# Layer norms and router statistics of a four-layer transformer kernel: from whole-tensor passes to one statistics and one scaling instruction per 128-row tile

## The chip, the cores and the metric

The kernel runs on one core of a Trainium2 chip. The metric is the device time of one execution in microseconds, and a kernel's time is the median of several executions. TensorE (PE) multiplies matrices, VectorE (DVE), ScalarE (ACT) and GpSimd (POOL) work on tiles of 128 partitions, and SyncE (SP) issues the transfers between memory and the on-chip buffer.

## The reference

Input x is 8 x 256 rows of 128 float32 numbers, with a context of the same shape. Four layers follow each other; each adds a gated attention over the context and a gated feed-forward part, both of a layer norm of x:

```python
def _layernorm(x, axis=-1, eps=1e-05):
    m = jnp.mean(x, axis=axis, keepdims=True)
    v = jnp.var(x, axis=axis, keepdims=True)
    return (x - m) / jnp.sqrt(v + eps)
...
    x = x + jnp.tanh(g_xattn[0]) * _L0_xattn_ref(_layernorm(x, axis=-1), ctx_1024, ctx_1024)
...
    x = x + jnp.tanh(g_ffn[3]) * _L3_ffn_ref(_layernorm(x, axis=-1), L3_ffn_r1_w, L3_ffn_r1_b, L3_ffn_r2_w, L3_ffn_w_up, L3_ffn_w_down, L3_ffn_a_up, L3_ffn_a_down)
```

Layer 0's feed-forward part is a chain of six attention nodes with a layer norm of its own (eps 1e-6) at its end. Layer 1's attention norms its input once more. The feed-forward parts of layers 1 and 2 are quantised. Layer 3's is a mixture of 32 experts, whose router sees each row beside six statistics of it:

```python
    def _stats(x):
        mean = x.mean(-1, keepdims=True)
        std = jnp.std(x, axis=-1, keepdims=True, ddof=1)
        mn = x.min(-1, keepdims=True)
        mx = x.max(-1, keepdims=True)
        l2 = jnp.linalg.norm(x, axis=-1, keepdims=True)
        sp = (jnp.abs(x) < 1e-06).astype(x.dtype).mean(-1, keepdims=True)
        return jnp.concatenate([mean, std, mn, mx, l2, sp], -1)
```

## The kernel before

x stays in the buffer for the whole run as X, 128 partitions x 16 tiles x 128 columns (NT = 16, D = 128), one row of x per partition and tile. Each part of a layer is a stage, written once for each engine as a function (l0f_dve, l1x_dve, ffn_dve, x_dve, moe_dve and their counterparts). Stages are separated by barriers that all five engines reach. Inside a stage the order of the work is written by hand, and engines wait on semaphores. On VectorE, link() adds to a semaphore when an instruction ends and waits for it before the next starts; an instruction without link() is followed by the next one with no wait.

A stage begins with its loads, issued by SyncE right after the barrier, and with the norm of X into Qf on VectorE. Meanwhile GpSimd and ScalarE fill blank rows of the query and key buffers (L342 and L347) once all loads have landed. TensorE then transposes Qf and goes on with the stage.

The norm is ln_dve, called nine times: at the start and the end of layer 0's node chain, twice in layer 1's attention, once in each of the two quantised feed-forward parts, in layer 2's and layer 3's attention, and in the router's stage. It makes five passes over 2048 numbers a partition (L311, L313, L314, L315, L317), and calls rstd_dve (L287 to L296), which asks ScalarE for a square root (L301) and improves its inverse by one Newton step. The norm of layer 0's attention is made from another layout by other code and doesn't call ln_dve. The router's stage then computes the mean, the deviation and the 2-norm of every row of Qf with six more passes (L1923 to L1930), asks ScalarE for the roots, and goes on with the minimum (L1932), the maximum (L1933) and the count of small values.

Of the kernel before, what the change touches and what calls it, by code (L numbers as in the profile page):

```python
# [18 lines left out]
P = 128  # L19
B, S, D = 8, 256, 128  # L20
NT = B * S // P
# [119 lines left out]
def flamingo(nc, T, out):  # L141
    with ExitStack() as ctx:
        def sb(name, shape, dt=F32, scope=ctx):
            return scope.enter_context(nc.sbuf_tensor(name, shape, dt))
# [35 lines left out]
        rest = sb("rest", [P, 2 * S])  # L180
        st1 = sb("st1", [P, 256])
# [121 lines left out]
        def bc(ap, shape):  # L303
            return ap.to_broadcast(shape)

        def ln_dve(v, src, dst, tmp, eps):

            d = v.eng
            sh = [P, NT, D]
            m = st1[:, 0:NT]  # L310
            v.link(d.tensor_reduce(m, src, AX, ALU.add))  # L311
            v.link(d.tensor_scalar(m, m, -1.0 / D, None, ALU.mult))
            v.link(d.tensor_tensor(dst, src, bc(m.unsqueeze(2), sh), ALU.add))  # L313
            v.link(d.tensor_tensor(tmp, dst, dst, ALU.mult))  # L314
            v.link(d.tensor_reduce(m, tmp, AX, ALU.add))  # L315
            rstd_dve(v, m, NT, eps, 1.0 / D)
            v.link(d.tensor_tensor(dst, dst, bc(st3[:, 0:NT].unsqueeze(2), sh), ALU.mult))  # L317

# [660 lines left out]
        def l0f_dve(v):  # L982
            d = v.eng
            ln_dve(v, X[:], Qf[:], O[:], 1e-5)
# [11 lines left out]
            ln_dve(v, Qf[:], Qf[:], O[:], 1e-6)  # L996
# [231 lines left out]
        def l1x_dve(v):  # L1228
            d = v.eng
            ln_dve(v, X[:], Qf[:], O[:], 1e-5)  # L1230
            ln_dve(v, Qf[:], Qf[:], O[:], 1e-5)
# [137 lines left out]
        def ffn_dve(v, Q):  # L1369
# [4 lines left out]
            ln_dve(v, X[:], Qf[:], O[:], 1e-5)  # L1374
# [252 lines left out]
        def x_dve(v, k):  # L1627
            d = v.eng
            L = attentions[k]
            ln_dve(v, X[:], Qf[:], O[:], 1e-5)  # L1630
# [285 lines left out]
        def moe_dve(v):  # L1916
            d = v.eng
            ln_dve(v, X[:], Qf[:], O[:], 1e-5)
            sh = [P, NT, D]
            mean, dev = st[:, :, 0:1], col[:, 2, :]  # L1920

            v.link(d.memset(st[:], 1.0))
            v.link(d.tensor_reduce(st[:, :, 0], Qf[:], AX, ALU.add))  # L1923
            v.link(d.tensor_scalar(st[:, :, 0], st[:, :, 0], 1.0 / D, None, ALU.mult))
            v.link(d.tensor_tensor(O[:], Qf[:], bc(mean, sh), ALU.subtract))
            v.link(d.tensor_tensor(O[:], O[:], O[:], ALU.mult))
            v.link(d.tensor_reduce(col[:, 2], O[:], AX, ALU.add))
            v.link(d.tensor_scalar(col[:, 2], col[:, 2], 1.0 / (D - 1), None, ALU.mult))
            v.link(d.tensor_tensor(O[:], Qf[:], Qf[:], ALU.mult))
# [280 lines left out]
```

## Time and profile before

| | us |
|---|---|
| median of 3 runs | 1986.42 (1985.71 to 1988.87) |
| the profiled execution | 1996.73 |
| its span | 1994.8 |
| TensorE busy | 1377.0 |
| VectorE busy | 1362.2 |
| ScalarE busy | 752.7 |
| GpSimd busy | 410.0 |

The span goes from the first to the last instruction of the profiled execution, whose own time includes what lies around it. Busy times add up what an engine works anywhere in the span; they don't say which engine the others wait for in a given stage.

### The profile page before, as it was taken

To read this page: it belongs to the slowest core of one execution; us is meant where nothing else is said; L and a number is where in the kernel's file an instruction comes from. 1 tells how busy PE (TensorE), PEld (TensorE's weight loads), DVE (VectorE), ACT (ScalarE), POOL (GpSimd) and SP (SyncE) were. 2 spreads that over 40 slices of the span, in tenths; PEclk is the share of its full clock that TensorE was granted. 3 is DMA by queue.
4 is the path that set the end of the run, shared out by engine and by line. 5 is a ranking of instruction groups with operands and counts; after the bars stand their busy time and mean duration, and the time that the engine had idled before them with its cause. 6 is when DMAs were issued, how large, how long until landed. Compare 5 with 4: busy or idle time off the path is not lost. (4 is left out here: it accounts for less than half of the span.)

```text
span 1994.8 us, 32063 instructions
## 1 busy us (share of the span) xinstructions
PE 1377.0 (69%) x12362; PEld 955.8 (48%) x12362; DVE 1362.2 (68%) x2054; ACT 752.7 (38%) x1092; POOL 410.0 (21%) x588
## 2 busy tenths in 40 slices
PE   0798189999999933888888834299514887120997
PEld 0565156666666621555665522166404454110897
DVE  5564457777777766676777778476587675869565
ACT  1255147667777731333333312145321365100110
POOL 6243232222222100222222200434102100000221
PEclk9898589999999975899999965589757799555899
DMA  2242322222232201000000000222001320110342
GB/s 69 49 68 35 92 81 88 83 89 89 85 91 85 89 24 41 1 1 1 1 1 1 1 11 0 48 60 53 12 0 32 65 50 19 61 21 0 93 146 86
DMA packets 115183, 95.88 MB, mean 48 GB/s; under 512 B 44180, under 2 KB 98516, under 8 KB 114132
## 3 DMA queue, kind: packets, MB, share of 16 engines
q1 hardware_dynamic: 114020, 92.63, 17.5%
q8 instruction: 96, 1.57, 0.3%
q0 software_dynamic: 1024, 1.32, 0.3%
q14 instruction: 43, 0.35, 0.1%
HBM read 33.23 MB, written 3.15 MB: 18 GB/s over the span
## 5 line engine op out<-in xcount | busy, mean ns | idle before, releaser
L586 ACT ACTIVATE Pt<-bank 128x1024 f32<-128x1024 f32 (+1 forms) x384 | 366.1, 953 | 181.0 <-PE bank L530 179.3
L642 DVE TENSOR_REDUCE l0f_Mf<-bank 128x4 f32<-128x1024 f32 x192 | 234.5, 1222 | 108.1 <-PE bank L509 108.0
L550 PE MATMUL bank<-Pt,V 128*32 128x256 f32 (+1 forms) x3072 | 199.0, 378 | 10.1 <-POOL Pt L391 8.9
L1102 POOL TENSOR_TENSOR Psum<-Pt 128x512 f32<-128x512 f32 x64 | 81.1, 1267 | 321.7 <-ACT Pt L1221 321.7
L550 PEld LDWEIGHTS bank<-Pt,V 128*32 128x32 f32 x3072 | 82.2, 112 | 82.8 <-issue 29.4
L832 PE MATMUL bank<-ident,Qf 128*128 128x128 f32 x64 | 14.1, 414 | 154.4 <-SPq L242 91.5
L391 POOL TENSOR_SCALAR_AFFINE_SELECT Pt<-Pt 128x512 f32<-128x512 f32 x128 | 81.5, 637 | 181.0 <-ACT Pt L586 181.0
L1269 DVE RECIPROCAL st<-bank 128x256 f32<-128x256 f32 x64 | 111.9, 1749 | 6.9 <-PE bank L1182 6.8
L1244 DVE TENSOR_TENSOR qk_lo<-bank,qk_hi 128x512 fp32r<-128x512 f32 x64 | 44.1, 689 | 103.2 <-ACT qk_hi L1213 103.2
L530 PE MATMUL bank<-l0f_QK 64*128 64x256 f32 x768 | 97.6, 333 | 19.8 <-DMA l0f_QK<-l0f_NMrow 19.2
L407 POOL CAST parts<-nodes 128x256 fp32r<-128x256 f32 x96 | 38.0, 396 | 305.1 <-PE bank L481 305.1
L642 DVE TENSOR_REDUCE l2x_Mf<-bank 128x4 f32<-128x1024 f32 x64 | 76.8, 1220 | 32.7 <-PE bank L509 32.7
L1764 POOL DMA_INDIRECT xg<-s_rows,sloti x32 | 29.3, 916 | 330.1 <-PEq L242 237.9
L1221 ACT ACTIVATE Pt<-bank 128x1024 f32<-128x1024 f32 x64 | 65.5, 1024 | 77.7 <-PE bank L1165 77.7
L530 PEld LDWEIGHTS bank<-l0f_QK 64*128 64x128 f32 x768 | 57.9, 187 | 73.2 <-ACT Pt L586 34.0
L832 PEld LDWEIGHTS bank<-ident,Qf 128*128 128x128 f32 x64 | 12.9, 224 | 155.3 <-SPq L242 92.2
L1177 PE MATMUL bank<-Pt,V 128*64 128x256 f32 x512 | 70.3, 395 | 19.6 <-DVE AnT L1271 19.6
L509 PE MATMUL bank<-l0f_QK 63*128 63x256 f32 x768 | 78.6, 283 | 5.8 <-DVE l0f_Mf L642 5.8
L1213 ACT CAST qk_hi<-bank 128x512 fp32r<-128x512 f32 x64 | 37.5, 586 | 115.0 <-PE bank L1121 115.0
L1248 DVE TENSOR_REDUCE Mx<-bank 128x4 f32<-128x1024 f32 x64 | 77.8, 1216 | 1.0 <-PE bank L1140 1.0
L590 ACT COPY OT<-bank 128x512 f32<-128x512 f32 x96 | 56.2, 586 | 54.6 <-PE bank L550 54.6
L559 PE MATMUL bank<-ident,OT 128*128 128x128 f32 x384 | 63.3, 289 | 13.0 <-ACT OT L590 5.5
(363 smaller groups left out, 3383.7 us busy)
## 6 DMA issues: line engine op xcount, KB each, us to landing
l0f_QK<-l0f_Z SPq DMA_DIRECT2D x288, 128.0 KB, 2.4
l2x_QK<-l2x_Z SPq DMA_DIRECT2D x96, 128.0 KB
Wup<-in_L_upT SPq DMA_DIRECT2D x16, 512.0 KB, 3.5
l0x_QK<-l0x_Z SPq DMA_DIRECT2D x48, 128.0 KB
Wdn<-in_L_downT SPq DMA_DIRECT2D x16, 256.0 KB, 3.6
Aup<-in_L_aupT SPq DMA_DIRECT2D x16, 128.0 KB, 3.5
l0f_QK<-l0f_NMrow SPq DMA_DIRECT2D x96, 4.0 KB
WeT<-in_L_WeT SPq DMA_DIRECT2D x1, 1280.0 KB
```

Of the source, the lines that this page charges most:

```text
L391: e.affine_select(diagonal, diagonal, [[0, 2], [0, 2], [1, P]], ALU.is_ge, 0.0, base=0, channel_multiplier=-1).then_inc(L.kept, 1)
L509: last = pe.matmul(bank[L.first(j) + x][:, t * S:t * S + w], L.QK[rs, u % L.ring, j, 0, t * P:(t + 1) * P], L.QK[rs, u % L.ring, j, 1, 0:w ...
L530: last = pe.matmul(bank[2 + x][:, t * S:t * S + S - q0], L.QK[rs, u % L.ring, j, 1, t * P:(t + 1) * P], L.QK[rs, u % L.ring, j, 0, q0:S], ...
L550: last = pe.matmul(bank[4][32 * x:32 * x + 32, o + q0:o + S], Va[:, 2 * n + k, 4 * j + x, :], Pp[:, (f + x // 2) % 4, x % 2, k * S:k * S + ...
L559: last = pe.transpose(b[:, (2 * t + k) * P:(2 * t + k + 1) * P], OT[:, k, t * P:(t + 1) * P], ident[:, :])
L586: act.activation(Pp[:, g % 4, :, 0:w], banks[:, 2:4, 0:w], ACT.Exp, scale=L.scale).then_inc(exp_done, 1)
L642: d.tensor_reduce(m, A.rearrange("p h (t k) -> p h t k", t=2), AX, ALU.max).then_inc(max_done, 1)
L1102: e.tensor_tensor(Psum[:, q % 2], Pp[:, q % 4, :, 0:S], Pp[:, q % 4, :, S:2 * S], ALU.add).then_inc(key_sum, 1)
L1177: pe.matmul(y[64 * x:64 * x + 64, 0:S], Vr[:, u % 8, k, 2 * j + x, :], Pp[:, g % 4, x, k * S:(k + 1) * S], start=(k == 0), stop=(k == 1), ...
L1221: act.activation(Pp[:, g % 4], banks[:, 2:4, :], ACT.Exp, scale=float(DH1) ** -0.5).then_inc(l1_exp, 1)
L1248: d.tensor_reduce(m[:, :, 2 * j:2 * j + 2].rearrange("p t h -> p h t"), banks[:, 0:2, :].rearrange("p h (t k) -> p h t k", t=2), AX, ALU.m ...
L1269: d.reciprocal(st1[:], y[:, S:2 * S]).then_inc(pair_done, 1)
```

## The change

A norm now begins with `moments`: one BN_STATS instruction for each of the 16 tiles, which writes six numbers a row (for the even and for the odd columns apart: a count, their mean, and their sum of squared deviations), and five small instructions that combine them to twice the mean and the variance. After rstd_dve, which is the same, one tensor_scalar a tile subtracts the mean and multiplies by the inverse root; both operands are read from a column of numbers, one for each partition. The 16 instructions of either kind have no wait between them. The norm no longer uses the scratch tensor O. The router's mean, deviation and 2-norm come from the same `moments` and five small instructions.

```diff
+        bn = sb("bn", [P, NT, 6])
...
-        def ln_dve(v, src, dst, tmp, eps):
+        def moments(v, src):
...
             d = v.eng
-            sh = [P, NT, D]
-            m = st1[:, 0:NT]
-            v.link(d.tensor_reduce(m, src, AX, ALU.add))
-            v.link(d.tensor_scalar(m, m, -1.0 / D, None, ALU.mult))
-            v.link(d.tensor_tensor(dst, src, bc(m.unsqueeze(2), sh), ALU.add))
-            v.link(d.tensor_tensor(tmp, dst, dst, ALU.mult))
-            v.link(d.tensor_reduce(m, tmp, AX, ALU.add))
-            rstd_dve(v, m, NT, eps, 1.0 / D)
-            v.link(d.tensor_tensor(dst, dst, bc(st3[:, 0:NT].unsqueeze(2), sh), ALU.mult))
...
+            for t in range(NT):
+                last = d.bn_stats(bn[:, t, :], src[:, t, :])
+            v.link(last)
+            m, dif, var = st1[:, 0:NT], st1[:, NT:2 * NT], st1[:, 2 * NT:3 * NT]
+            d.tensor_tensor(m, bn[:, :, 1], bn[:, :, 4], ALU.add)
+            d.tensor_tensor(dif, bn[:, :, 1], bn[:, :, 4], ALU.subtract)
+            v.link(d.tensor_tensor(var, bn[:, :, 2], bn[:, :, 5], ALU.add))
+            v.link(d.scalar_tensor_tensor(out=dif, in0=dif, scalar=0.25, in1=dif, op0=ALU.mult, op1=ALU.mult))
+            v.link(d.scalar_tensor_tensor(out=var, in0=var, scalar=1.0 / D, in1=dif, op0=ALU.mult, op1=ALU.add))
+            return m, var
+
+        def ln_dve(v, src, dst, eps):
+
+            d = v.eng
+            m, var = moments(v, src)
+            d.tensor_scalar(m, m, 0.5, None, ALU.mult)
+            rstd_dve(v, var, NT, eps, 1.0)
+            for t in range(NT):
+                last = d.tensor_scalar(dst[:, t, :], src[:, t, :], m[:, t:t + 1], st3[:, t:t + 1], ALU.subtract,
+                                       ALU.mult)
+            v.link(last)
...
         def moe_dve(v):
             d = v.eng
-            ln_dve(v, X[:], Qf[:], O[:], 1e-5)
-            sh = [P, NT, D]
-            mean, dev = st[:, :, 0:1], col[:, 2, :]
-
+            ln_dve(v, X, Qf, 1e-5)
             v.link(d.memset(st[:], 1.0))
-            v.link(d.tensor_reduce(st[:, :, 0], Qf[:], AX, ALU.add))
-            v.link(d.tensor_scalar(st[:, :, 0], st[:, :, 0], 1.0 / D, None, ALU.mult))
-            v.link(d.tensor_tensor(O[:], Qf[:], bc(mean, sh), ALU.subtract))
-            v.link(d.tensor_tensor(O[:], O[:], O[:], ALU.mult))
-            v.link(d.tensor_reduce(col[:, 2], O[:], AX, ALU.add))
-            v.link(d.tensor_scalar(col[:, 2], col[:, 2], 1.0 / (D - 1), None, ALU.mult))
-            v.link(d.tensor_tensor(O[:], Qf[:], Qf[:], ALU.mult))
-            v.link(d.tensor_reduce(col[:, 3], O[:], AX, ALU.add))
+            m, var = moments(v, Qf)
+            v.link(d.tensor_scalar(st[:, :, 0], m, 0.5, None, ALU.mult))
+            v.link(d.tensor_scalar(col[:, 2], var, float(D) / (D - 1), None, ALU.mult))
+            v.link(d.tensor_tensor(col[:, 3], st[:, :, 0], st[:, :, 0], ALU.mult))
+            v.link(d.tensor_tensor(col[:, 3], col[:, 3], var, ALU.add))
+            v.link(d.tensor_scalar(col[:, 3], col[:, 3], float(D), None, ALU.mult))
             d.drain().then_inc(ln_ask, 1)
```

On VectorE, the norm at the start of layer 1's feed-forward part stands in a row before as follows (st is any of the small buffers st1 to st3, Qf the normed rows, O the scratch tensor):

```order
L311 TENSOR_REDUCE st<-X 128x16
L312 TENSOR_SCALAR st<-st 128x16
L313 TENSOR_TENSOR Qf<-X,st 128x2048
L314 TENSOR_TENSOR O<-Qf 128x2048
L315 TENSOR_REDUCE st<-O 128x16
L287 TENSOR_SCALAR st<-st 128x16
L288 COPY st<-st 128x16
L292 RECIPROCAL st<-st 128x16
L293 TENSOR_TENSOR st<-st 128x16
L294 TENSOR_TENSOR st<-st 128x16
L295 TENSOR_SCALAR st<-st 128x16
L296 TENSOR_TENSOR st<-st 128x16
```

It ends with one more pass, L317. In the changed kernel the same place reads, on the same engine (line numbers of the changed kernel; bn holds the six numbers a row and tile):

```order
L311 BN_STATS bn<-X 128x6 x16
L314 TENSOR_TENSOR st<-bn 128x16
L315 TENSOR_TENSOR st<-bn 128x16
L316 TENSOR_TENSOR st<-bn 128x16
L317 SCALAR_TENSOR_TENSOR st<-st 128x16
L318 SCALAR_TENSOR_TENSOR st<-st 128x16
L325 TENSOR_SCALAR st<-st 128x16
L288 TENSOR_SCALAR st<-st 128x16
L289 COPY st<-st 128x16
L293 RECIPROCAL st<-st 128x16
```

Four passes of 2048 and one small instruction became 16 statistics and six small ones ahead of the root; behind it, the pass L317 became 16 instructions L328. Next, VectorE in the router's stage before, from the setting of the statistics' buffer on (col holds columns of per-row numbers):

```order
L1922 MEMSET st 128x128
L1923 TENSOR_REDUCE st<-Qf 128x16
L1924 TENSOR_SCALAR st<-st 128x16
L1925 TENSOR_TENSOR O<-Qf,st 128x2048
L1926 TENSOR_TENSOR O<-O 128x2048
L1927 TENSOR_REDUCE col<-O 128x16
L1928 TENSOR_SCALAR col<-col 128x16
L1929 TENSOR_TENSOR O<-Qf 128x2048
L1930 TENSOR_REDUCE col<-O 128x16
L1932 TENSOR_REDUCE st<-Qf 128x16
```

And there in the changed kernel, with the norm's last instructions ahead:

```order
L328 TENSOR_SCALAR Qf<-X,st 128x128 x16
L1928 MEMSET st 128x128
L311 BN_STATS bn<-Qf 128x6 x16
L314 TENSOR_TENSOR st<-bn 128x16
L315 TENSOR_TENSOR st<-bn 128x16
L316 TENSOR_TENSOR st<-bn 128x16
L317 SCALAR_TENSOR_TENSOR st<-st 128x16
L318 SCALAR_TENSOR_TENSOR st<-st 128x16
L1930 TENSOR_SCALAR st<-st 128x16
L1931 TENSOR_SCALAR col<-st 128x16
L1932 TENSOR_TENSOR col<-st 128x16
L1933 TENSOR_TENSOR col<-col,st 128x16
```

Six passes of 2048 and two small instructions ahead of the minimum became 16 statistics and ten small ones; the minimum and all that follows stay. No other engine's instructions change.

## Rows read from the trace of the kernel before

**Rows 1.** The page, busy time, share of the span and instructions of each engine.

```profile
PE 1377.0 (69%) x12362; PEld 955.8 (48%) x12362; DVE 1362.2 (68%) x2054; ACT 752.7 (38%) x1092; POOL 410.0 (21%) x588
```

**Rows 2.** Windows: length, busy us of PE, PEld, DVE, ACT, POOL, clock, DMA share, GB/s.

```profile
210.00:242.00 32.00, 0.00 (x0) 0.00 (x0) 18.20 (x20) 5.38 (x6) 10.07 (x18) 0.50 0.50 140
...
743.00:774.00 31.00, 0.00 (x0) 0.00 (x0) 29.35 (x27) 1.92 (x4) 8.13 (x4) 0.50 0.31 104
...
1694.00:1736.00 42.00, 0.00 (x0) 0.00 (x0) 38.95 (x35) 1.73 (x3) 0.00 (x0) 0.52 0.19 73
```

**Rows 3.** Timeline, layer 1's feed-forward: start us, duration us, instruction.

```profile
1165.65 2.29 DVE L311 TENSOR_REDUCE st<-X 128x16 f32<-128x2048 f32 x1
...
1167.97 0.17 DVE L312 TENSOR_SCALAR st<-st 128x16 f32<-128x16 f32 x1
...
1175.15 0.17 DVE L287 TENSOR_SCALAR st<-st 128x16 f32<-128x16 f32 x1
...
1175.66 1.28 ACT L301 ACT_TABLE_LOAD   x1 [11.17 <-DVEq L289]
...
1178.33 2.29 DVE L317 TENSOR_TENSOR Qf<-Qf,st 128x2048 f32<-128x2048 f32 x1
...
1180.76 2.29 DVE L1377 TENSOR_REDUCE top<-Qf 128x1 f32<-128x2048 f32 x1
```

**Rows 4.** Timeline of VectorE, router's stage.

```profile
1709.62 2.29 DVE L1923 TENSOR_REDUCE st<-Qf 128x16 f32<-128x2048 f32 x1
...
1724.09 2.29 DVE L1932 TENSOR_REDUCE st<-Qf 128x16 f32<-128x2048 f32 x1
1726.29 2.28 DVE L1933 TENSOR_REDUCE st<-Qf 128x16 f32<-128x2048 f32 x1
...
1760.02 1.59 DVE L1972 MAX8 t<-pr 128x8 f32<-128x32 f32 x16
```

**Rows 5.** Groups of instructions of VectorE: busy us, mean ns of one, idle before.

```profile
L1932 DVE TENSOR_REDUCE st<-Qf 128x16 f32<-128x2048 f32 x1 | 2.3, 2287 | 0.1
...
L1972 DVE MAX8 t<-pr 128x8 f32<-128x32 f32 x16 | 1.6, 177 | 0.0
...
L1967 DVE TENSOR_REDUCE col<-pr 128x16 f32<-128x512 f32 x1 | 0.7, 685 | 0.8 <-ACT pr L1886 0.8
...
L1439 DVE TENSOR_SCALAR diag<-ident,sw,gates 128x128 f32<-128x128 f32 x2 | 0.7, 345 | 0.1
```

**Rows 6.** Timeline, start of layer 3's attention.

```profile
1506.48 2.29 DVE L311 TENSOR_REDUCE st<-X 128x16 f32<-128x2048 f32 x1
...
1514.62 5.57 POOL L342 CAST l2x_QK<-l2x_rowk 128x2048 fp32r<-128x2048 f32 x3 [6.96 <-DMA l2x_rowk<-in_c_rows]
...
1516.57 1.80 DVE L288 COPY st<-st 128x16 f32<-128x16 f32 x1
...
1520.87 2.29 DVE L317 TENSOR_TENSOR Qf<-Qf,st 128x2048 f32<-128x2048 f32 x1
```

**Rows 7.** Timeline, start of layer 0's node chain.

```profile
231.23 2.29 DVE L317 TENSOR_TENSOR Qf<-Qf,st 128x2048 f32<-128x2048 f32 x1
...
232.46 4.92 POOL L342 CAST l0f_QK<-l0f_rowk 128x1024 fp32r<-128x1024 f32 x4 [12.96 <-DMA V<-in_L_ffn_We]
...
233.55 2.92 DVE L988 TENSOR_TENSOR ewbe<-ew,beT 128x1 f32<-128x1 f32 x6
```

**Rows 8.** Timeline, start of layer 2's attention.

```profile
1269.69 2.29 DVE L1654 TENSOR_TENSOR X<-X,bx 128x2048 f32<-128x2048 f32 x1
...
1273.91 7.13 POOL L1589 TENSOR_SCALAR padr<-padi 16x2048 fp32r<-16x2048 int32 x1 [7.55 <-issue]
```

**Rows 9.** Timeline, start of layer 1's attention.

```profile
745.86 1.89 POOL L1091 TENSOR_TENSOR Esel<-Esel,ident 128x1024 bf16<-128x1024 bf16 x1
746.22 1.56 DVE L312 TENSOR_SCALAR st<-st 128x16 f32<-128x16 f32 x1
...
750.14 3.87 DVE L314 TENSOR_TENSOR O<-Qf 128x2048 f32<-128x2048 f32 x1
```

More of the change, by code:

```diff
@@ L995, in l0f_dve @@
             v.barrier()
-            ln_dve(v, Qf[:], Qf[:], O[:], 1e-6)
+            ln_dve(v, Qf, Qf, 1e-6)
             sh_ = [P, NT, D]
@@ L1229, in l1x_dve @@
             d = v.eng
-            ln_dve(v, X[:], Qf[:], O[:], 1e-5)
-            ln_dve(v, Qf[:], Qf[:], O[:], 1e-5)
+            ln_dve(v, X, Qf, 1e-5)
+            ln_dve(v, Qf, Qf, 1e-5)
             loaded(v, 8)
@@ L1373, in ffn_dve @@
             top = {"apply_absolute_value": Q.gated}
-            ln_dve(v, X[:], Qf[:], O[:], 1e-5)
+            ln_dve(v, X, Qf, 1e-5)
             loaded(v, len(ffn_loads(Q)))
@@ L1629, in x_dve @@
             L = attentions[k]
-            ln_dve(v, X[:], Qf[:], O[:], 1e-5)
+            ln_dve(v, X, Qf, 1e-5)
             loaded(v, len(x_loads(k)))
@@ L1917, in moe_dve @@
             d = v.eng
-            ln_dve(v, X[:], Qf[:], O[:], 1e-5)
-            sh = [P, NT, D]
-            mean, dev = st[:, :, 0:1], col[:, 2, :]
+            ln_dve(v, X, Qf, 1e-5)
             v.link(d.memset(st[:], 1.0))
-            v.link(d.tensor_reduce(st[:, :, 0], Qf[:], AX, ALU.add))
-            v.link(d.tensor_scalar(st[:, :, 0], st[:, :, 0], 1.0 / D, None, ALU.mult))
-            v.link(d.tensor_tensor(O[:], Qf[:], bc(mean, sh), ALU.subtract))
-            v.link(d.tensor_tensor(O[:], O[:], O[:], ALU.mult))
-            v.link(d.tensor_reduce(col[:, 2], O[:], AX, ALU.add))
-            v.link(d.tensor_scalar(col[:, 2], col[:, 2], 1.0 / (D - 1), None, ALU.mult))
-            v.link(d.tensor_tensor(O[:], Qf[:], Qf[:], ALU.mult))
-            v.link(d.tensor_reduce(col[:, 3], O[:], AX, ALU.add))
+            m, var = moments(v, Qf)
[4 more added lines that the diff above has]
+            v.link(d.tensor_scalar(col[:, 3], col[:, 3], float(D), None, ALU.mult))
             d.drain().then_inc(ln_ask, 1)
```

## The prediction

> **What bounds the kernel now.** The page comes first [rows 1]: TensorE is busy 69% of the span and VectorE 68%, and neither share says what a layer norm is worth. So I cut the span at the stage borders and read it by windows [rows 2]. In the stretches where the norms stand TensorE is idle: 0.00 us of work between 743 and 774 us and between 210 and 242 us, 0.00 between 1694 and 1736 us. In two of the three VectorE is busy nearly throughout (29.35 of 31 us, 38.95 of 42 us). There VectorE alone sets the end: every microsecond taken off it is a microsecond of the kernel. In 210 to 242 it works 18.20 of 32 us, so something else ends that stretch. I then went through the timeline of all nine calls of ln_dve and asked of each which engine arrives last at the barrier that follows.
>
> Six calls end a stretch alone: the one after the node flow (722 us), both of the first cross stage (744 and 761 us), both feed-forward ones (1166 and 1434 us) and the router's (1694 us). [rows 3] is one of them: each instruction starts 0.03 to 0.04 us after the end of the one before, nothing is hidden under it, and the maximum of L1377 follows at once. The eighth (1506 us) ends its part too, but shares it with GpSimd. Two don't count: the call at 218 us ends at 233.5, while GpSimd's casts, which had to wait for the weights, begin only at 232.46 [rows 7]; and the one at 1251 us is over long before GpSimd's L1589, which starts at 1273.91 and takes 7.13 us while VectorE's last work ends at 1271.98 [rows 8].
>
> **The change part by part.** *Removed from a norm.* From the first instruction to L287 it is 1175.15 - 1165.65 = 9.50 us [rows 3], for two sums, a subtraction and a product over 2048 elements, and a small one. L317 is 2.29 + 0.03 = 2.32 us. Together 11.82 us. What lies between, rstd_dve, stays: 1178.33 - 1175.15 = 3.18 us with ScalarE's table load.
>
> *Sixteen statistics instructions.* The trace has none, so I bound them. They have no semaphore between them, and what such a chain costs is its start-to-start distance, not the duration. Two unlinked sums show it: L1932 starts at 1724.09 and L1933 at 1726.29, 2.20 us apart, though each lasts 2.29 [rows 4]. The slope is 1.04 ns an element (2.287 us for 2048 less 0.685 for 512, over 1536 [rows 5]), so 0.067 of the 2.20 us is fixed. The 16 maxima of 32 elements take 1.59 us, 177 ns each but (1.59 - 0.18)/15 = 94 ns apart, which is 33 + 61 [rows 4, 5]. So 128 elements at one a cycle give 0.133 + 0.067 = 0.20 us, and 16 of them 3.20 + 0.09 of tail + 0.03 = 3.32 us. Lower bound: 0.19 with the maxima's 61 ns. Upper bound: two cycles an element, as if one pass took the mean and one the variance, 0.333 us each. I take the low end: the nearest rows, a sum and an 8-fold maximum over one input, both run at one element a cycle.
>
> *The small ones.* Two unlinked on 16 values at 0.067 + 0.017 = 0.08, three linked at 0.21 (0.17 of L312 [rows 3] and 0.04 to the next), one unlinked 0.08: 0.87 us. First instruction to L287: 4.19 us instead of 9.50, a gain of 5.31.
>
> *Sixteen tensor_scalar with two pointer operands.* One of this very shape and operands stands in the trace: L1439, 345 ns with a wait on either side [rows 5]. In a chain I take off the 2.29 - 2.20 = 0.09 of overlap: 0.26 us, times 16, + 0.12 = 4.28 us. It replaces 2.32. This half of the change loses 1.96 us a norm: the 16 fixed parts and 32 pointer loads cost more than the saved pass of 2048. Bounds: 0.26 and, with no overlap, 0.345.
>
> Net per exposed norm: 5.31 - 1.96 = 3.35 us; six of them 20.1.
>
> *Router's statistics.* L1923 starts at 1709.62 and L1932 at 1724.09 [rows 4]: 14.47 us for six passes and two small ones. New: 3.32 for the statistics, 0.79 for two unlinked and three linked small ones, five linked small ones at 0.21, 0.1 of drain: 5.26. Gain 9.2 us, all on the path (ScalarE's root is asked for earlier, and VectorE still has its minima, maxima and counts to do behind it).
>
> *Contention with GpSimd.* Sums run undisturbed beside GpSimd's work, while VectorE's two-input, copy and tensor_scalar instructions take turns with it: at 746 us L312 lasts 1.56 instead of 0.17 us and L314 3.87 instead of 2.29 [rows 9], 2.97 us together. The new statistics have one input and should go through, until (746.22 - 2.32) + 3.32 = 747.2; then the small ones wait for L1091 until 747.75 and for one more turn of 1.89: 2.4 us. Gain 0.5 more.
>
> At 1506 us the turns cost more. The load-bound casts L342 start at 1514.62 and last 5.57 us [rows 6]; L288 waits 1.80 there. New: the moments end at 1506.48 + 4.19 = 1510.67, the root without table load (3.18 - 1.28) leads to 1512.57, and (1514.62 - 1512.57)/0.26 = 8 of the 16 products are done when the casts begin. The six small ones of L988 in 2.92 us beside three casts show that two unlinked instructions pass per cast [rows 7], so some 4 are left at 1520.6 and the norm ends near 1521.8 instead of 1523.2: gain 1.4. Bounds: 0, and 1523.2 - (1512.57 + 4.28) = 6.3 if these products don't take turns at all.
>
> *The two covered calls.* At 218 us GpSimd's first cast waits for L317 until 233.52, 1.06 us [rows 7]; the norm is now over by 231, gain 1.0. Were that cover gone, this norm would be worth 3.35. At 1251 us the products now fall on GpSimd's casts instead of into the gap between them and L1589; each turn delays GpSimd by some 0.2 us, and GpSimd ends that stretch: loss 0.6, between 0 and 2.3 (if L1654, 2.29 us, gets in ahead of GpSimd's copy) [rows 8].
>
> What is late next in the first cross stage are the loads. The DMA engines are busy 0.31 of the 31 us there [rows 2], 9.6 us, so they are through long before the new barrier at about 767.
>
> **Sum.** 20.1 + 9.2 + 0.5 + 1.4 + 1.0 - 0.6 = 31.6 us. The profiled execution took 1996.73 us, 10.3 above the median of the three runs, with the same stretches; nothing in the sum depends on TensorE. Profile: 1965.1. Median: 1986.4 - 31.6 = **1954.8 us**.
>
> **A rule that speaks against it.** The Trainium skill, page "VectorE: DVE Perf Modes", section "The DRAIN you can't avoid", says that the next instruction starts only when the pipe has emptied, semaphore or not, and that the number of instructions is what to minimise; its section on the trn2 errata adds that many small tiles pay the fixed cost each. This trace disagrees for unlinked instructions, 94 ns apart at 177 ns each. The page "Vector Engine (DVE) Microarchitecture Reference", section 5.2, gives about 75 ns an instruction after overlap; an estimate from it would be 0.133 + 0.075 = 0.208 us for one statistics instruction, 1 us more over the kernel.
>
> **Rivals.** (a) *The chain doesn't overlap.* Statistics 0.286 us each (the sum's 2.286 less 1920 x 1.042 ns), products 0.345. A norm: 16 x 0.286 + 0.03 + 0.87 + 16 x 0.345 + 0.03 = 11.04 against 11.82, gain 0.8; router 7.8; the casts at 1514 then catch nearly all products, gain 0 there. 4.7 + 7.8 + 0.5 + 1.0 - 0.6 = 13.4: 1973.0 us. The maxima [rows 4, 5] speak against it; that a pointer load may end the overlap speaks for its half. By the Trainium skill's drain rule above, this is what would come. Chance 0.10.
> (b) *Two cycles an element.* 16 x 0.133 = 2.13 us more in seven exposed places, and the 1.4 at 1506 us goes: 31.6 - 16.3 = 15.3, 1971.1 us. No row excludes it. Chance 0.11.
> (c) *More than forecast.* The products pass GpSimd freely, 6.3 instead of 1.4 us at 1506, and nothing is lost at 1251: 1986.4 - 31.6 - 4.9 - 0.6 = 1949.3 us. The waits of L288 speak against. Chance 0.10.
> (d) *Slower.* The statistics instruction has a long fixed part of its own. It decides at 31.6/(7 x 16) = 0.28 us more each, from 0.48 us a piece; at 0.6 us it is 112 x 0.40 = 45 us, 2000 us. Nothing in the trace is near that (the short instructions stand at 0.15 to 0.35 us isolated), but the instruction is unseen. Chance 0.04.
>
> My case: 0.65, own range 1948 to 1962. Under 0.2%, 4 us, a measurement of this kernel can't tell a difference; a statistics instruction of 0.44 to 0.52 us, between (b) and (d), would land there, 0.03 out of these two. The range takes in (a), (b) and (c): 1947 to 1974. Faster 0.94, same 0.03, slower 0.03.
>
> **What would show it.** In the profile after: BN_STATS mean under 0.3 us, 16 of them in 3.3 us; L328 mean about 0.345, 16 in 4.3; first statistics to L288 4.2 us; TensorE's first transpose of the gated feed-forward 3.4 us earlier after its stage's start; the router's stretch from the norm's end to the minima 5.3 us; the start-up to 242 us only 1 us shorter. Wrong it would be above all if 16 statistics take 5 us or more.

## The result, and the profile after

The changed kernel takes 1957.13 us (median of 4 executions, 1952.78 to 1959.63) against 1987.53 of before in the same rounds: a ratio of 0.9838, 95% interval 0.9818 to 0.9858, or 28 to 36 us less. A second series on another occasion gave 1958.34 us and 0.9848 (0.9812 to 0.9885). The prediction was 1954.8. Of all executions reported here one, of the kernel that takes the statistics twice, stood at a granted clock of 0.62 and took 2287.92 us; it is left out of that kernel's median and ratio.

The page's busy line of the kernel after, beside [rows 1]:

```profile
PE 1365.0 (70%) x12362; PEld 947.0 (49%) x12362; DVE 1325.6 (68%) x2360; ACT 753.7 (39%) x1092; POOL 413.4 (21%) x588
```

VectorE has 306 instructions more and 36.6 us of work less. Its share of the span is 68% as before, since the span has shrunk with it.

The timeline of VectorE in the kernel after, layer 1's feed-forward, the counterpart of [rows 3]:

```profile
1149.06 3.19 DVE L311 BATCH_NORM_STATS2 bn<-X 128x6 f32<-128x128 f32 x16
1152.29 0.18 DVE L314 TENSOR_TENSOR st<-bn 128x16 f32<-128x16 f32 x1
...
1153.20 0.17 DVE L288 TENSOR_SCALAR st<-st 128x16 f32<-128x16 f32 x1
...
1156.38 4.19 DVE L328 TENSOR_SCALAR Qf<-X,st 128x128 f32<-128x128 f32 x16
1160.72 2.29 DVE L1386 TENSOR_REDUCE top<-Qf 128x1 f32<-128x2048 f32 x1
```

From the first statistics to L288 it is 1153.20 - 1149.06 = 4.14 us; the same piece was 9.50 us. The 16 instructions L328, called the products from here on, take 4.19 us in a row.

The groups of VectorE in the kernel after, each form apart: busy us, mean ns of one, idle before.

```profile
L328 DVE TENSOR_SCALAR Qf<-X,st 128x128 f32<-128x128 f32 x112 | 40.9, 442 | 0.3
...
L311 DVE BATCH_NORM_STATS2 bn<-X 128x6 f32<-128x128 f32 x112 | 22.3, 278 | 1.0
...
L328 DVE TENSOR_SCALAR Qf<-Qf,st 128x128 f32<-128x128 f32 x32 | 8.4, 338 | 0.1
```

A statistics instruction lasts 278 ns, yet 16 of them end after 3.19 us: they start (3.19 - 0.28)/15 = 0.194 us apart. The product lasts 338 ns where nothing disturbs it, and starts (4.19 - 0.34)/15 = 0.257 us apart. The 442 ns of the group on X come from the two attention norms that meet GpSimd's casts, where the 16 products take 10.84 us (layer 2) and 9.14 us (layer 3).

The timeline of VectorE in the router's stage of the kernel after, beside [rows 4]:

```profile
1675.13 3.19 DVE L311 BATCH_NORM_STATS2 bn<-Qf 128x6 f32<-128x128 f32 x16
...
1680.04 0.17 DVE L1934 TENSOR_SCALAR col<-col 128x16 f32<-128x16 f32 x1
1680.36 2.29 DVE L1936 TENSOR_REDUCE st<-Qf 128x16 f32<-128x2048 f32 x1
```

The statistics up to the minimum take 1680.36 - 1675.13 = 5.23 us instead of 14.47.

The first rows of layer 1's attention in the kernel after, where [rows 9] showed VectorE taking turns with GpSimd:

```profile
735.45 3.19 DVE L311 BATCH_NORM_STATS2 bn<-X 128x6 f32<-128x128 f32 x16
738.68 0.68 DVE L314 TENSOR_TENSOR st<-bn 128x16 f32<-128x16 f32 x1
...
739.57 1.76 DVE L317 SCALAR_TENSOR_TENSOR st<-st 128x16 f32<-128x16 f32 x1
```

The 16 statistics pass undisturbed; two small ones wait for their turn, 0.50 + 1.59 = 2.09 us instead of 2.97.

Read stretch by stretch over the same instructions of both traces, from the first instruction of the norm to the first work of TensorE or GpSimd that waits for it (in layer 2's attention, to GpSimd's first copy ahead of TensorE; for the norm that ends the node chain, to the next stage's first load), in us:

| stretch | before | after | gain | forecast |
|---|---|---|---|---|
| start-up norm to the transposes | 23.86 | 22.84 | 1.0 | 1.0 |
| norm that ends the node chain | 22.10 | 18.62 | 3.5 | 3.35 |
| both norms of layer 1's attention | 30.42 | 22.59 | 7.8 | 7.2 |
| gated feed-forward | 29.61 | 26.15 | 3.5 | 3.35 |
| layer 2's attention | 30.50 | 30.46 | 0.0 | -0.6 |
| plain feed-forward | 28.75 | 25.28 | 3.5 | 3.35 |
| layer 3's attention | 16.94 | 15.43 | 1.5 | 1.4 |
| router's norm and statistics | 41.66 | 28.95 | 12.7 | 12.55 |
| sum | | | 33.5 | 31.6 |

The two profiled spans differ by more, 1994.8 - 1951.1 = 43.7 us. The other 10.2 lie in stretches whose code is the same: 5.9 ahead of the first norm, 4.8 and 1.2 in the flows of layers 2 and 3, 0.3 in layer 1's, less 1.9 given back in the node chain. Before's profiled execution lies 9 us above its median and after's 4 below, which is enough for that part; most likely it belongs to the two executions and not to the change.

### The profile page after: what moved, and what is told of

It reads as the page before. It is cut to its first block and busy times, and to the rows that moved or that the text cites. A ratio compares the mean times of both kernels' runs of the same rounds, so it can differ in the third digit from the quotient of the medians.

```text
span 1951.1 us, 32369 instructions
## 1 busy us (share of the span) xinstructions
PE 1365.0 (70%) x12362; PEld 947.0 (49%) x12362; DVE 1325.6 (68%) x2360; ACT 753.7 (39%) x1092; POOL 413.4 (21%) x588
## 5 line engine op out<-in xcount | busy, mean ns | idle before, releaser
L559 PE MATMUL bank<-Pt,V 128*32 128x256 f32 (+1 forms) x3072 | 194.8, 372 | 11.1 <-POOL Pt L400 10.0
L418 POOL TENSOR_TENSOR parts<-nodes,parts 128x256 fp32r<-128x256 f32 x96 | 70.2, 731 | 7.7
```

Source lines behind the costliest of these rows:

```text
L418: e.tensor_tensor(lo, node, hi.bitcast(F32), ALU.subtract).then_inc(L.parts_in, 1)
L559: last = pe.matmul(bank[4][32 * x:32 * x + 32, o + q0:o + S], Va[:, 2 * n + k, 4 * j + x, :], Pp[:, (f + x // 2) % 4, x % 2, k * S:k * S + ...
```

## The experiments

Each was timed beside the kernel before on one chip, in four series on different chips; so medians of different series are best compared by their ratios to before. Where a few microseconds decide I read TensorE's idle gap around a norm, from the end of its last work ahead of the norm to its first work behind it. Over the same code the gap mostly repeats to 0.03 us between executions (cross stage, that is the node chain's last norm and both of layer 1's attention: 42.14, 42.17, 42.15; gated feed-forward 26.98, 27.00, 27.00), with one exception of 0.4 us (42.53 in the cross stage of the kernel with the covered norms as before); in layer 2's attention, where loads end late, it moves by a microsecond. Whole executions of one kernel spread by 10 to 20 us.

**The router alone.** The edit, against the changed kernel: every call of the norm goes to the old function, the router's part stays as changed.

```diff
-            ln_dve(v, X, Qf, 1e-5)
+            ln_dve(v, X[:], Qf[:], O[:], 1e-5)
```

> The router's statistics as in the changed kernel, all layer norms as before. The prediction priced this half at 9.2 us, the changed kernel's trace gives it 14.47 - 5.23 = 9.2: about 1978 us against 1987.5. If the instructions of a chain did not overlap it would be 7.8. If the two halves of the change help each other (one shortens what the other waits for), this run and the norms' 24 us do not add up to the 30 us measured. In the trace: L323's group absent, the sixteen statistics of the router in 3.2 us, and the norms' L312 to L317 with their durations of before.

Measured: 1983.74 us, ratio 0.9965 (0.994 to 0.999), 2 to 12 us faster. The router's gap is 33.35 instead of 42.59 us, 9.24 less, to the hundredth what the changed trace gave; the cross stage's 53.79 and the feed-forward's 30.45 stay as in the kernel before (53.80, 30.45). The overlap-free 7.8 is out. From 33.35 the norm takes the router's gap to the changed kernel's 29.88, another 3.47, so the halves add up: they don't help each other.

**Whole-tensor passes.**

```diff
-            d.tensor_scalar(m, m, 0.5, None, ALU.mult)
+            v.link(d.tensor_scalar(m, m, 0.5, None, ALU.mult))
+            v.link(d.tensor_tensor(dst[:], src[:], bc(m.unsqueeze(2), sh), ALU.subtract))
             rstd_dve(v, var, NT, eps, 1.0)
-            for t in range(NT):
-                last = d.tensor_scalar(dst[:, t, :], src[:, t, :], m[:, t:t + 1], st3[:, t:t + 1], ALU.subtract,
-                                       ALU.mult)
-            v.link(last)
+            v.link(d.tensor_tensor(dst[:], dst[:], bc(st3[:, 0:NT].unsqueeze(2), sh), ALU.mult))
```

> The statistics instruction stays; subtraction and product are two passes over all 2048 elements again, one ahead of the root and one behind it. Theory of the prediction: sixteen instructions cost 4.2 us in the changed kernel's trace, two passes 2 x 2.32 = 4.65 us, of which none lies under ScalarE's root because the subtraction stands ahead of it; so this kernel is 0.4 us slower than the changed one at each of six or seven exposed norms, and about 1960 us. Rival: the sixteen fixed parts and 32 pointer loads make 'one instruction a tile' a loss (it looks like one if only the product pass of 2.32 us is compared); then this kernel is faster than the changed one, at or below 1955.

Measured: 1958.5 us, 0.9859 (0.9824 to 0.9894), not to be told from the changed kernel by its time. The first matmul behind each kernel's gated feed-forward norm, with TensorE's idle time before it in brackets; first the kernel after, then this one:

```profile
1175.39 0.82 PE L1501 MATMUL bank<-identb,xq 128*128 128x128 bf16 x6 [26.98 <-SPq L243]
```

```profile
1176.60 0.60 PE L1500 MATMUL bank<-identb,xq 128*128 128x128 bf16 x4 [27.53 <-SPq L243]
```

The whole passes cost 0.55 us more a norm (0.56 in the plain feed-forward, 1.69 over the three norms of the cross stage), of which some 0.1 is the link behind the small L325's counterpart. So the one instruction a tile is worth a little, and the statistics are worth nearly all: the 1.96 us that the prediction booked as a loss of this half is the product alone, and the subtraction's 2.32 that goes with it was booked with the moments.

**Every instruction linked to the one before.**

```diff
             for t in range(NT):
-                last = d.bn_stats(bn[:, t, :], src[:, t, :])
-            v.link(last)
+                v.link(d.bn_stats(bn[:, t, :], src[:, t, :]))
```

and the same for the products.

> Same instructions as the changed kernel, but a semaphore wait on the one before between every two statistics and every two products. Theory of overlap: the distance grows from 0.194 to 0.276 + 0.035 = 0.31 us for a statistics instruction and from 0.257 to 0.339 + 0.035 = 0.37 for a product, 15 x 0.117 + 15 x 0.117 = 3.5 us a norm, six exposed norms 21 us, the router 1.8, the norm at 1478 us about 1.5: some 24 us more than the changed kernel, 1981 us. Rival, that the next instruction starts only when the one before has left the pipe, link or no link: only the semaphore's 0.035 us is added, 30 x 0.035 = 1.05 us a norm and 0.5 in the router, some 7 us in all, 1964.

Measured: 1990.05 us, 1.001 (0.9988 to 1.0033). Its timeline of VectorE, gated feed-forward:

```profile
1158.88 5.21 DVE L311 BATCH_NORM_STATS2 bn<-X 128x6 f32<-128x128 f32 x16
...
1168.22 6.08 DVE L327 TENSOR_SCALAR Qf<-X,st 128x128 f32<-128x128 f32 x16
1174.45 2.29 DVE L1384 TENSOR_REDUCE top<-Qf 128x1 f32<-128x2048 f32 x1
```

Sixteen statistics take 5.21 instead of 3.19 us and sixteen products 6.08 instead of 4.19, which is 0.329 and 0.383 us apart instead of 0.194 and 0.257. The gaps grow by 3.92 (gated), 3.93 (plain), 5.96 (router), 10.12 (cross stage) and, from stage start, 3.3 and 0.6 to 1.2 in layers 3 and 2: 28 us, where 24 were expected. Without the overlap of unlinked instructions the whole change would be worth about 5. The rival's 7 us is out. The rule of the Trainium skill, page "VectorE: DVE Perf Modes", section "The DRAIN you can't avoid", that chaining instructions without semaphores saves nothing, does not hold here: 0.194 against 0.329 us apart. The same section says beside it that an instruction that isn't held starts earlier, and that is what the trace shows. The median lies 33 us over the changed kernel, some 5 more than the gaps say (and 9 over the 1981 expected); the last experiments are about such remainders.

**The statistics twice.**

```diff
+            for t in range(NT):
+                last = d.bn_stats(st2[:, 128 + 6 * t:134 + 6 * t], src[:, t, :])
             for t in range(NT):
                 last = d.bn_stats(bn[:, t, :], src[:, t, :])
```

> Sixteen more statistics instructions ahead of each set, into a buffer that nobody reads (extra work only). If they are on the path and 0.194 us apart, each exposed set adds 16 x 0.194 = 3.1 us: seven of them 21.7, and 1 to 1.5 us at the attention norm that meets GpSimd's casts; the start-up and the norm at 1231 us add nothing. So about 22 to 24 us over the changed kernel, 1980 us. If the real price were 0.276 us each (no overlap between independent ones), 31 us. If much less than 20 appears, the norms are less exposed than the stretches say.

Measured: 1990.79 us (median of 11), ratio 0.9998 (0.9971 to 1.0025), which by the ratio is about 1988 us, where 1980 was expected. Its timeline in the gated feed-forward (the view ends after three of the second sixteen), and its first matmul behind:

```profile
1146.25 3.19 DVE L311 BATCH_NORM_STATS2 st<-X 128x6 f32<-128x128 f32 x16
1149.35 0.66 DVE L313 BATCH_NORM_STATS2 bn<-X 128x6 f32<-128x128 f32 x3
...
1175.67 1.14 PE L1503 MATMUL bank<-identb,xq 128*128 128x128 bf16 x9 [30.08 <-SPq L243]
```

1149.35 - 1146.25 = 3.10 us for sixteen, and the gap grows by 3.10 (30.08 - 26.98): all of them are on the path. Likewise 3.10 in the plain feed-forward and 6.20 in the router. In the cross stage it is 7.21 and not 9.3, because the moments' small instructions now come after GpSimd has finished and the 2.09 us of turns vanish: 9.30 - 2.09 = 7.21. With 2.8 in layer 3's stage the stretches add 22, as expected. The time rose by about 31, so some 9 us lie elsewhere.

**The covered norms as before.**

```diff
+            if k == 2:
+                ln_old(v, X[:], Qf[:], O[:], 1e-5)
+            else:
+                ln_dve(v, X, Qf, 1e-5)
```

and the old norm, here named ln_old, at start-up too.

> The norms at the start-up and ahead of the third attention stage as before the change, all else as changed. The prediction calls both covered, the first by GpSimd's casts (worth 1.0 us), the second by GpSimd's last transposition (worth -0.6, 0.0 measured in the changed trace). So +1 us on the changed kernel, that is no difference in the median, and TensorE's gaps there 37.7 and 33.6 us long as in the kernel before. If each were exposed, +3.5 us each, +7. For the second stage: if the sixteen small products taking turns cost GpSimd time, its gap is shorter here than in the changed kernel (37.4).

Measured, with the changed kernel in the same rounds:

> The changed kernel once more, on the same chip and in the same rounds as the three that follow, because executions of one kernel lie up to 20 us apart here and go with the granted clock (0.01 of it is 14 us). Expected: 1957 again, ratio 0.984 or a little over; TensorE's idle gaps around the norms 218 us in sum, of before 251.

The changed kernel 1958.34 us, 0.9848 (0.9812 to 0.9885); with the two old norms 1961.08 us, 0.9855 (0.9819 to 0.9891): no difference beyond the measurement. The start-up's gap is 38.04 against 37.03 and 36.74, so 1.0 to 1.3 us, as the covering casts allow. Layer 2's attention takes from its first instruction to TensorE's first 31.45 us with the old norm and 32.01 and 32.61 with the new. Counted from GpSimd's first cast, which moves by up to 1.2 us with the loads, it is 22.96 against 23.38 and 23.43. But the kernel before and the one with the router alone, both with the old norm there, have 23.81 and 23.28, so a difference between the norms is not shown.

**Subtraction under ScalarE's root.** The whole passes, but with the subtraction behind the request for the root and ahead of the wait for it:

```diff
             d.drain().then_inc(ln_ask, 1)
+            if meanwhile:
+                meanwhile()
             d.wait_ge(ln_answer, v.count("ln"))
...
+            def meanwhile():
+                v.link(d.tensor_tensor(dst[:], src[:], bc(m.unsqueeze(2), sh), ALU.subtract))
```

> The statistics as changed; the subtraction is one pass of 2048 elements issued while ScalarE takes the root, and one product pass follows. VectorE waits 1.68 us for ScalarE where a table must be loaded, so 2.32 us of subtraction cost 0.64 there, and the product pass saves 4.22 - 2.32 = 1.90: 1.3 us less than the changed kernel in each of the four norms with a table load (both feed-forward, the node one's follower and the router's), about nothing in the others: -5 us, 1952. If VectorE's time is all that counts (no overlap with ScalarE), it is +0.4 a norm as with both passes behind each other.

Measured: 1963.58 us, 0.9864 (0.9818 to 0.9909). The gaps give 0.97 us a norm in both feed-forwards and the router. In the cross stage they give 0.3: 0.97 for the norm that ends the node chain, less 0.68 for the two of layer 1's attention, where ScalarE has no table to load and the root is there early. The overlap is there, 0.3 less than expected: the root's answer is taken up 0.79 us later instead of 0.64, and one more link costs 0.12. Layer 3's attention gains 3.0 us (12.46 from stage start against 15.43 and 15.45): the last pass gets in after one turn. Layer 2's loses 3.2 to 3.8. Its timeline there:

```profile
1241.98 9.45 POOL L354 CAST l2x_QK<-l2x_rowk 128x2048 fp32r<-128x2048 f32 x3 [7.39 <-DMA l2x_rowk<-in_c_rows]
1243.99 1.79 DVE L1665 TENSOR_SCALAR bx<-bx,gates 128x128 f32<-128x128 f32 x1
1245.82 3.87 DVE L1666 TENSOR_TENSOR X<-X,bx 128x2048 f32<-128x2048 f32 x1
...
1260.35 7.13 POOL L1601 TENSOR_SCALAR padr<-padi 16x2048 fp32r<-16x2048 int32 x1 [7.08 <-issue]
```

The three casts take 9.45 us and not 5.57, since whole VectorE passes of 2.29 us now fall between them, and GpSimd ends this stretch. That is more than the 2.3 us that the prediction gave as its upper bound for the changed kernel here. The median misses the expected 1952 by some 11 us; its six executions fall into 1954.2 to 1957.4 and 1969.8 to 1972.4, and the profiled one, of the upper three, has the longer last segment described below.

**The product shared with ScalarE.**

```diff
+        DVE_TILES = 10
...
+            a.eng.wait_ge(ln_ask, a.count("ln"))
+            for t in range(DVE_TILES, NT):
+                last = a.eng.activation(Qf[:, t, :], src[:, t, :], ACT.Identity, scale=st3[:, t:t + 1],
+                                        bias=st1[:, 4 * NT + t:4 * NT + t + 1])
+            last.then_inc(ln_answer, 1)
...
+            v.link(d.scalar_tensor_tensor(out=st1[:, 4 * NT:5 * NT], in0=m, scalar=-1.0, in1=st3[:, 0:NT],
+                                          op0=ALU.mult, op1=ALU.mult))
+            d.drain().then_inc(ln_ask, 1)
-            for t in range(NT):
+            for t in range(DVE_TILES):
...
+            d.wait_ge(ln_answer, v.count("ln"))
```

> The products are shared: VectorE takes ten tiles, ScalarE six (multiply and add with a column each), and VectorE waits for ScalarE at the end. VectorE saves 6 x 0.257 = 1.54 us, and one linked small instruction and the hand-over add about 0.4. So 1.1 us less an exposed norm, 8 us in all, 1949, if ScalarE's six take under 2.6 us. Rival: ScalarE needs over 0.45 us a tile with the hand-over or loads another table, and the norm is longer than before its division: a gain of nothing or a loss.

Measured: 1954.49 us, 0.9829 (0.9787 to 0.9872). Its timeline of ScalarE, gated feed-forward:

```profile
1146.29 2.42 ACT L310 ACTIVATE Qf<-X,st 128x128 f32<-128x128 f32 x6 [1.41 <-DVEq L339]
1148.72 1.28 ACT L1561 ACT_TABLE_LOAD   x1
1150.02 0.20 ACT L1561 ACTIVATE clip<-clip 128x2 f32<-128x2 f32 x1
```

Six tiles take 2.42 us, less than VectorE's ten. The gap shrinks by 1.21 in the plain feed-forward and 1.22 in the router, a little more than the 1.1 expected. In the gated one it shrinks by 0.06: the table for the clip's factors (L1561) was loaded while VectorE multiplied, and now comes behind ScalarE's share, so the barrier waits for ScalarE instead. Over the three norms of the cross stage it shrinks by 2.43, where 3.3 were expected: 1.2 for each of the first two and nothing for the third, behind which ScalarE loads a table for the gate in the same way:

```profile
753.90 1.28 ACT L1233 ACT_TABLE_LOAD   x1
755.20 0.20 ACT L1233 ACTIVATE g<-g 128x1 f32<-128x1 f32 x1
```

TensorE starts at 755.50. With 1.4 in layer 3's stage and 1.0 to 1.5 in layer 2's it is some 7.5 us in all.

**A form for each place.**

```diff
+            ln_dve(v, X, Qf, 1e-5, "wait" if Q.gated else "split")
...
+            ln_dve(v, X, Qf, 1e-5, "wait" if k == 3 else "split")
```

where wait is the subtraction under the root, split the shared product; start-up and router stay as changed.

> At each norm the form whose stretch was shortest so far: the shared product (ten tiles VectorE, six ScalarE) after the node flow, in the first cross stage, in the third attention stage and in the plain feed-forward stage; the subtraction under ScalarE's root in the gated feed-forward and the fourth attention stage; start-up and router as in the changed kernel. From TensorE's gaps of the two experiments against the changed kernel: 2.44 + 1.0 + 1.23 + 0.98 + 3.0 = 8.7 us less, gap of the router 29.9 as in the changed one and with it the clock of the stage after it as there: 1957.5 - 8.7 = 1949. Rival: the clock takes back a part in another stage, 1950 to 1960.

Measured: 1945.35 us (1942.74 to 1956.28), ratio 0.9782 (0.9757 to 0.9808), the lowest median of all: 43 us under before, where the changed kernel has 31. The gaps are 39.69 in the cross stage, 26.02, 25.17 and 29.88; layer 3's stage is 1.4 us shorter than in the changed kernel and not 3.0, layer 2's no shorter (32.14): 6.0 us by the stretches, where 8.7 were expected. In layer 3's stage the casts began 7.93 us after the stage's start, ahead of the last small instruction, which had to wait; with the same form they had begun 8.17 us after it, just behind that instruction, in the kernel with the subtraction under the root everywhere:

```profile
1482.29 7.62 POOL L378 CAST l2x_QK<-l2x_rowk 128x2048 fp32r<-128x2048 f32 x3 [6.75 <-DMA l2x_rowk<-in_c_rows]
1482.40 1.81 DVE L299 TENSOR_TENSOR st<-st 128x16 f32<-128x16 f32 x1
1484.24 3.92 DVE L344 TENSOR_TENSOR Qf<-Qf,st 128x2048 f32<-128x2048 f32 x1
```

So a quarter of a microsecond in the landing of a load decided over 1.6 us there. The median lies 12 to 13 us under the changed kernel's two (11 to 13 by the ratios), more than the stretches account for. And by the stretches this kernel saves less than the product shared everywhere (7.5); that its median is 9 us lower (the intervals of the two ratios overlap) goes with the clock behind the router, the subject of the next part.

**Where the remainders come from.** The stretches of the shared product said some 7.5 us less than the changed kernel and the median shows 4; doubled statistics said +22 and show about +31. Windows of three kernels after the router's gap: the second 10 us of the stage, 20 us around the start of the experts' matmuls, and the whole rest; columns as in [rows 2]. The kernel after (gap 29.88):

```profile
1702.28:1712.28 10.00, 9.29 (x40) 5.84 (x40) 0.00 (x0) 3.06 (x4) 0.00 (x0) 0.83 0.00 0
1802.28:1822.28 20.00, 17.34 (x82) 15.71 (x83) 7.45 (x20) 2.97 (x8) 4.51 (x5) 0.60 0.19 63
...
1692.28:1951.10 258.82, 158.33 (x978) 135.74 (x978) 173.10 (x352) 26.66 (x78) 29.40 (x32) 0.78 0.22 67
```

The shared product (gap 28.66):

```profile
1687.22:1697.22 10.00, 9.32 (x18) 2.64 (x16) 0.00 (x0) 3.05 (x4) 0.00 (x0) 0.54 0.00 0
1787.22:1807.22 20.00, 11.70 (x46) 10.32 (x47) 7.23 (x16) 2.48 (x6) 4.87 (x5) 0.50 0.06 12
...
1677.22:1949.80 272.58, 171.41 (x978) 144.50 (x978) 173.18 (x352) 26.64 (x78) 29.32 (x32) 0.73 0.21 63
```

The same 978 matmuls take 272.58 us instead of 258.82. In the kernel after, TensorE's granted clock is at 0.83 in the second ten microseconds, mostly at 2.4 GHz; with the shared product it has fallen to 0.54, nearly all of it at 1.2 GHz (this is called the early fall below), so that only 18 matmuls get done instead of 40, and the experts' work starts 5.6 us later and at the lower clock. Three runs ask whether the length of the gap decides this, or chance. The first two add passes to the router's stretch, the third shares the router's product too:

```diff
+            v.link(d.tensor_reduce(st2[:, 128:128 + NT], Qf[:], AX, ALU.add))
```

```diff
+            for n in (NT, NT, 12):
+                v.link(d.tensor_reduce(st2[:, 128:128 + n], Qf[:, 0:n], AX, ALU.add))
```

```diff
-            ln_dve(v, X, Qf, 1e-5, "plain")
+            ln_dve(v, X, Qf, 1e-5)
```

> The kernel with the shared product and one more pass of 2.3 us in the router's stretch, a sum over 2048 elements that nobody reads (extra work only). In the profiles so far TensorE's granted clock after the router's stretch takes one of two courses over the same instructions: where the gap was 29.9, 30.4, 33.4 or 42.6 us the expert stage is 12 to 14 us shorter than where it was 28.7, 28.9, 35.8 or 36.1. Theory: this goes with the length of the gap, by kernel and not by chance. Then here, with a gap of 28.7 + 2.3 = 31.0, the extra work makes the kernel faster: +2.3 - 13, from 1954.5 to about 1944, the last segment (from the router's norm on) 285 instead of 296 us. Rival, that the course is drawn anew in each execution: +2.3, 1957.

Measured: 1953.89 us, 0.9809 (0.9789 to 0.9828), where 1944 was expected; gap 30.98; 261.5 us from the first matmul to the end.

> The changed kernel with three more passes in the router's stretch, sums over 2048, 2048 and 1536 elements that nobody reads (extra work only), 2.3 + 2.3 + 1.7 = 6.3 us, which puts the gap at 29.9 + 6.2 = 36.1 us, among those with the longer expert stage. Theory, that the course of the clock goes with the gap's length: +6.2 + 12 = 18 us on the changed kernel, about 1976, the last segment 302 us instead of 283.6. Rival, that it is drawn by chance: +6.2, 1964, segment 290.

Measured: 1973.54 us, 0.9915 (0.9898 to 0.9933), 15.8 over the mean of the changed kernel's two medians, or 13 to 15 by the ratios; gap 36.31, 268.5 us to the end.

> The kernel with a form by place, its router norm too with the product shared between VectorE and ScalarE. By the stretches alone this is 1.2 us faster (router's gap 28.7 instead of 29.9), 1944. Theory that the clock's course after the router goes with the gap's length: at 28.7 us the clock falls some 10 us into the stage and comes back 20 us later, as in the profiles with 28.7, 28.9 and 36 us, +13.5, so 1945.4 - 1.2 + 13.5 = 1958. Rival, the course is drawn by chance in each execution: 1944.

Measured: 1952.42 us, 0.9806 (0.9782 to 0.9829), between the theory's 1958 and the rival's 1944. It is 7 us slower than the same kernel with the plain router norm (the intervals of the two ratios overlap), although its stretches are 1.2 us shorter; gap 28.66, 264.1 us to the end. Windows of these three after the router's gap, the same stretches. The one more pass:

```profile
1702.18:1712.18 10.00, 9.32 (x30) 4.99 (x30) 0.00 (x0) 3.05 (x4) 0.00 (x0) 0.79 0.00 0
...
1692.18:1953.70 261.52, 161.07 (x978) 137.96 (x978) 173.06 (x352) 26.64 (x78) 29.32 (x32) 0.77 0.21 66
```

The three more passes on the changed kernel:

```profile
1715.77:1725.77 10.00, 9.32 (x17) 2.66 (x16) 0.00 (x0) 3.06 (x4) 0.00 (x0) 0.51 0.00 0
...
1705.77:1974.30 268.53, 168.09 (x978) 141.53 (x978) 173.15 (x352) 26.66 (x78) 29.41 (x32) 0.74 0.21 64
```

The form by place with the router's product shared too:

```profile
1697.73:1707.73 10.00, 9.32 (x18) 2.64 (x16) 0.00 (x0) 3.06 (x4) 0.00 (x0) 0.55 0.00 0
...
1687.73:1951.80 264.07, 163.19 (x978) 137.40 (x978) 173.07 (x352) 26.66 (x78) 29.41 (x32) 0.75 0.21 65
```

Over all fourteen profiles the fall follows the gap without exception:

| router's gap, us | clock in the second 10 us | first matmul to end, us |
|---|---|---|
| 28.66 to 28.91 (3 kernels) | 0.53 to 0.55 | 264.1, 272.0, 272.6 |
| 29.88 to 30.45 (5 profiles of 4 kernels) | 0.82 to 0.85 | 258.6 to 259.1 |
| 30.98 | 0.79 | 261.5 |
| 33.35, 42.59 | 0.85, 0.89 | 259.1, 258.8 |
| 35.83 to 36.31 (3 kernels) | 0.51 to 0.52 | 268.5, 271.8, 271.8 |

In the three runs that were forecast, a gap lengthened by 6.4 us and one shortened by 1.2 both brought the early fall, and one lengthened by 2.3 took it away. That fourteen profiles fall so by chance is hard to believe; but all kernels but one have a single profile, so that each of their executions takes the same course is not shown, and the two groups of executions of the subtraction under the root would fit a mixture. The linked kernel and the doubled statistics, at 35.83 and 36.07 us, have the early fall too, which is where the 5 and 9 us beyond their gaps can lie. The size doesn't hold: 5 to 14 us, because the moment when the clock comes back varies too (between 130 and 150 us of the stage it stood at 0.99 in the last of these runs and at 0.57 with the shared product alone). In the medians the three more passes show it, +15.8 (13 to 15 by the ratios) where +6.4 is work; the +7 where -1.2 is work goes the same way and is within the noise. The forecast gain of the one more pass doesn't show: the profile has it behind the router (272.6 to 261.5), but the medians are 1954.5 and 1953.9. In its profile layer 1's attention flow, from the second norm to the gated feed-forward's, took 402.9 us against 393.5 in the shared product's, at a granted clock of 0.93 against 0.96. From layer 1's first matmul to the gated feed-forward's norm the profiles fall into two groups over the same code, 383.2 to 385.1 us in three of them, the shared product's among these, and 389.4 to 392.6 in the other eleven. What sets that length was not tried.

## Why the prediction was right

**The bound.** That VectorE alone ends six stretches holds: each gap moved by what VectorE's instructions moved, for the double statistics to the hundredth. [rows 2] had 0.00 us of TensorE between 743 and 774 us; the kernel after has 0.00 between 735.45 and 758.04.

**Statistics.** Forecast 0.20 us apart, 16 in 3.32 with the tail; measured 0.194, 3.23. The choice of one element a cycle against two, "the nearest rows", was right, and the overlap read from the maxima [rows 4, 5] carried over to an unseen instruction. The maxima's 61 ns of fixed part was the better of the two estimates (0.133 + 0.061 = 0.194).

**Small ones.** Forecast 0.87, measured 1153.20 - 1149.06 - 3.23 = 0.91.

**Products.** Forecast 0.26 apart, 4.28; measured 0.257, 4.22. That it is a loss of 1.96 against the product pass alone was right (1.91), and that the loss is made good by the subtraction saved is what the whole passes show: with both counted, the products are 0.55 us a norm the shorter.

**Router.** Forecast 9.2, measured 9.24 in two kernels.

**Contention.** The forecast was 0.5 in the cross stage, with waits of 2.4 us; they were 2.09, a gain of 0.9. The Trainium skill, page "SBUF — State Buffer", section "SBUF: two separate sides", makes the port shared by VectorE and GpSimd an exclusive lock, which whoever starts first holds for its whole instruction; the rows agree for the two-input and tensor_scalar instructions, and the statistics took 3.19 us with and without GpSimd beside them. In layer 3's stage 16 products took 9.14 us instead of 4.19, and ended 15.2 us after the stage's start where 15.3 was forecast.

**Covered calls.** Start-up 1.0 as forecast. Layer 2's attention: -0.6 forecast, 0.0 between the two profiles, -0.45 against the old norm in the changed kernel, within what the loads' landing leaves open. The forecast put 0.2 us of GpSimd's time on each turn, for which it named no row; beside all sixteen products the three casts and the copy behind them took 5.76 + 1.95 instead of 5.57 + 1.89 us, 0.25 in all.

**The mis-sized terms** are small and of one sign: 0.1 a norm, 0.4 of contention, 0.6 in layer 2's stage, 1.9 us in all, 33.5 instead of 31.6. The time gave back 30.4 and 27.5 in the two series. The difference is of the size of what TensorE's clock does behind the gaps, on which the sum said that nothing depends. That was the wrong sentence: with a router's gap 1.2 us shorter or 6 us longer the profiles show 5 to 14 us more behind it. That the changed kernel's gap of 29.88 us, like before's 42.59, was followed by no early fall was luck: nothing in the prediction could tell it, and with such a fall the time would have come out at some 1962 to 1971. The forecast of the profiled execution, 1965.1, missed the 1952.78 by 12 us, 10 of them in stretches whose code is the same and whose length the sum took as fixed. Rivals (a) and (b) are excluded by the linked kernel and by the 0.194; (c) by the 9.14 us of products at layer 3; (d) by the mean of 278 ns.

## What to carry to other kernels

Cost a chain of unlinked instructions by the distance between starts, not by duration, and look for any row in the trace with such a chain; put the semaphore on the last one only, where, as here, none of them reads what another writes. A pass that is moved to another engine or under a wait is worth what the barrier behind it shows: ask what the helper did in that time (a table load here) and who takes turns with it. Look at each place by itself: the shared product was the shortest form where ScalarE had nothing else to do (plain feed-forward, router), the subtraction under the root where it had (gated feed-forward). That the kernel with a form by place had the lowest median is no proof of it, since the clock behind the router gave more than the forms.

## What the runs showed of the hardware

The time of one kernel goes with its mean granted clock: over 29 executions of the kernel before, 1979.99 us to 2002.28, a straight line through time against clock falls by 14 us for each 0.01 and leaves 1.3 us of scatter. So nearly all of the spread between executions goes with how long TensorE's granted clock stood at the lower of its two levels.

Where the clock falls went, in these fourteen profiles, with the length of the idle gap before it, and not in one direction: 28.7 to 28.9 and 35.8 to 36.3 us end with the early fall, 29.9 to 33.4 and 42.6 us without it. A microsecond more or less in an idle stretch was thus followed by 5 to 14 us in the next one. What rule lies behind it no run here shows.
